# A fused attention and expert layer: few-row products padded to full height, and another stage order

## What is computed

```python
h = _L0_tok_ref(x, L0_tok_W, L0_tok_b, L0_tok_pos_emb)          # patches @ W.T + b + pos_emb
h = jnp.concatenate([h, txt], axis=1)                            # 249 tokens of 192
h = h + _L0_attn_ref(_layernorm(h, axis=-1), ...)                # 12 heads of 16, fq_act, log_int_softmax
h = h + _L0_ffn_ref(_layernorm(h, axis=-1), ...)                 # 16 experts of 128, 4 chosen, 1 shared
```

## Time and profile before

| | us |
|---|---|
| median of 3 runs | 3751.35 (3750.78 to 3755.88) |
| profiled execution, its own time | 3755.2 |
| span of the profile in it | 3753.5 |
| TensorE / VectorE / ScalarE / GpSimd busy | 3512.5 / 3529.2 / 3169.6 / 1378.5 |

### The profile page before, as it was taken

One profiled execution on the slowest core, in us unless ns is written; L12 is line 12 of the kernel. 1 busy time (PEld: TensorE's weight loads), 2 busy tenths in 40 slices (PEclk: granted clock), 3 DMA queues, 4 the chain that ended last, 5 costly groups with the idle time before them and its releaser, 6 DMA issues. The chain is left out here.

```text
span 3753.5 us, 97358 instructions
## 1 busy us (share of the span) xinstructions
PE 3512.5 (94%) x30764; PEld 2912.8 (78%) x30764; DVE 3529.2 (94%) x10282; ACT 3169.6 (84%) x6224; POOL 1378.5 (37%) x2219
## 2 busy tenths in 40 slices
PE   0269999999999999999999999999999999999999
PEld 0137888888888888888888888888888888888878
DVE  0579999999999999999999999999999999999995
ACT  0189889998998899899889989988998999899882
POOL 2033333434333343333334333333443343434330
PEclk9859999999999999999999999999999999999999
DMA  4100000000000000000000000000000000000000
GB/s 99 25 15 18 12 21 21 16 16 21 21 11 21 21 17 15 21 21 14 18 21 17 15 21 21 14 18 21 19 14 21 21 14 18 21 20 13 21 7 8
DMA packets 121213, 73.43 MB, mean 20 GB/s; under 512 B 15547, under 2 KB 118466, under 8 KB 120706
## 3 DMA queue, kind: packets, MB, share of 16 engines
q1 hardware_dynamic: 120706, 67.21, 7.1%
HBM read 54.89 MB, written 12.24 MB: 18 GB/s over the span
## 5 line engine op out<-in xcount | busy, mean ns | idle before, releaser
L1130 PE MATMUL pU<-x2T,UG 128*128 128x250 f16 x8704 | 1230.3, 270 | 0.3 <-DVE work L974 0.2
L1130 PEld LDWEIGHTS pU<-x2T,UG 128*128 128x128 f16 x8704 | 817.4, 97 | 124.3 <-DVE work L974 10.7
L1154 PE MATMUL pY<-WD,work 128*128 128x192 f32 (+1 forms) x4352 | 815.9, 329 | 0.0
L500 POOL TENSOR_SCALAR qz<-qk,quad,cst 128x249 bf16<-128x249 int8 x768 | 580.7, 769 | 549.5 <-ACT qk L605 541.7
L1154 PEld LDWEIGHTS pY<-WD,work 128*128 128x128 f32 (+1 forms) x4352 | 695.5, 187 | 20.9 <-DVE work L970 0.3
L913 DVE SCALAR_TENSOR_TENSOR work<-work,cst 128x249 f32<-128x249 f32 (+1 forms) x1536 | 676.7, 493 | 8.5 <-ACT work L576 7.5
L585 ACT ACTIVATE work<-work,alpha 128x249 f32<-128x249 f32 (+1 forms) x1536 | 643.7, 495 | 10.5 <-DVE work L934 3.3
L569 ACT ACTIVATE work<-a,room 128x249 bf16<-128x249 int8 (+1 forms) x1536 | 645.6, 504 | 0.8 <-POOL room L512 0.7
L1130 PE MATMUL pU<-x2T,UGB 67*128 67x250 f16 x2176 | 592.3, 272 | 0.0
L594 ACT ACTIVATE passing<-pX,cst 128x512 int16<-128x512 int16 (+3 forms) x768 | 475.6, 675 | 6.4 <-PE pO L1091 2.0
L512 POOL TENSOR_SCALAR room<-rmax,cst 128x4 f32<-128x4 f32 (+1 forms) x384 | 204.0, 531 | 745.2 <-DVE rmax L893 719.7
(11 more groups left out here) (201 smaller groups left out, 5832.8 us busy)
## 6 DMA issues: line engine op xcount, KB each, us to landing
img<-in_x_dram SPq DMA_DIRECT2D x896, 23.5 KB
img<-in_x_dram SPq DMA_DIRECT2D x768, 21.4 KB
h<-in_txt_dram SPq DMA_DIRECT2D x64, 96.0 KB, 1.9
out_dram<-yout SPq DMA_DIRECT2D x64, 96.0 KB
out_dram<-yout SPq DMA_DIRECT2D x64, 90.8 KB
WD<-in_L_ffn_Wd_dram SPq DMA_DIRECT2D x1, 1536.0 KB
work<-in_L_ffn_Wu_dram SPq DMA_DIRECT2D x2, 512.0 KB
work<-in_L_ffn_Wg_dram SPq DMA_DIRECT2D x2, 512.0 KB
```

Of the source, the lines that this page charges most:

```text
L500: nc_.tensor_scalar(qz[:, k * PER + m, :], qk8[:, k, :], quad[:, m:m + 1], cc(C_B0), ALU.mult, ALU.add)
L1130: a = mm(pU[:, s, q * EVEN:(q + 1) * EVEN], weights, x2T[i % 2][0:w, m, 0:EVEN], start=m == 0, stop=m == BLOCKS - 1)
L1154: a = mm(pY[0:n, t * 256:t * 256 + D], (act_[k % 2] if k else up[0])[:, c:c + n], WD[:, e, :], start=k == 0 and t == 0, stop=e == E - 1, s ...
```

## The change

It has two parts. First, products over few partitions are made products over more: `v_add`, `p_add` and `ones` become 128 partitions high (the added rows of `v_add` and `p_add` hold zeros, those of `ones` ones), `GW` gets a fourth block that holds the 64 last rows and zeros, so that `route` sums over 128 each time, and the last product of `embed` takes 116 partitions like the six ahead of it. GpSimd sets three more tensors to zero in the setup, and VectorE copies one more small block. `UGB` with its 67 partitions stays. Second, `ORDER` is another list with the same 251 stages. It was made from a table in which more stages may not stand beside GpSimd's. The list starts at another place of the cycle, so the shifts are one lower (down to -5).

```diff
-        v_add = sb("v_add", [SPLIT, D], BF16)
-        p_add = sb("p_add", [SPLIT, D], BF16)
+        v_add = sb("v_add", [P, D], BF16)
+        p_add = sb("p_add", [P, D], BF16)
...
-        ones = sb("ones", [SPLIT, P], BF16)
+        ones = sb("ones", [P, P], BF16)
...
-        GW = sb("GW", [P, 3, E], F16)
+        GW = sb("GW", [P, 4, E], F16)
...
-                      identf, ident, ident16, pick, ob, x2s, tokW_cols, UGB):
+                      identf, ident, ident16, pick, ob, x2s, tokW_cols, UGB, v_add, p_add, GW):
                 nc_.memset(a[:], 0.0)
...
+            link(ve.tensor_copy(GW[0:REST, 3, :], GW[0:REST, 1, :]))
...
-                            n = CROW + CK if 2 * c + 1 < K else CK
+                            n = CROW + CK
...
-                                w = P if m < BLOCKS - 1 else REST
-                                a = mm(pX[:, t * E:(t + 1) * E], x2T[i % 2][0:w, m, t * P:(t + 1) * P],
-                                       GW[0:w, (0, 1, 2, 0, 1)[m], :], start=m == 0, stop=m == BLOCKS - 1)
+                                a = mm(pX[:, t * E:(t + 1) * E], x2T[i % 2][:, m, t * P:(t + 1) * P],
+                                       GW[:, (0, 1, 2, 0, 3)[m], :], start=m == 0, stop=m == BLOCKS - 1)
```

More of the change, by code:

```diff
@@ L260, in fused_layer @@
         LATE_LOADS = E1 * SPLIT
-        VSETUP = 105
+        VSETUP = 106
         RT = 22
@@ L303, in fused_layer @@
         ORDER = [
[L304 to L352, removed]
+            ("imgload", 0, -1), ("gates", -4, -1), ("act", -5, 2), ("grow", -3, 1), ("mmU", -5, 4),
+            ("expo", -3, 3), ("turn", -2, 0), ("mmG", -5, 3), ("gate", -5, 3), ("turn", -2, 1),
@@ new lines, in fused_layer @@
+            ("low", -3, 3), ("quant", -2, 0), ("mmU", -5, 6), ("value", -3, 0), ("expo", -3, 5), ("qk", -2, 5),
+            ("share", -3, 4), ("value", -3, 1), ("qkq", -2, 5), ("r_top_pairs", -4, -1), ("top", -2, 0),
+            ("score", -2, 1), ("down", -5, 4), ("gate", -5, 5), ("silu", -5, 6), ("r_take_pairs", -4, -1),
+            ("grow", -3, 3), ("low", -3, 4), ("turnp", -3, 2), ("mmU", -5, 7), ("weigh", -3, 3),
+            ("quant", -2, 1), ("sum", -3, 5), ("pick", -5, 5), ("copyp", -3, 2), ("mmG", -5, 6), ("act", -5, 5),
@@ new lines, in fused_layer @@
+            ("turnp", -3, 3), ("peak", -2, 0), ("pick", -5, 6), ("alpha", -3, 5), ("r_penalty", -4, -1),
+            ("outq", -3, 0), ("score", -2, 2), ("outcast", -3, 0), ("below", -2, 0), ("copyp", -3, 3),
+            ("conv", -2, 2), ("down", -5, 5), ("top", -2, 1), ("quant", -2, 2), ("gate", -5, 6),
+            ("grow", -3, 4), ("mmG", -5, 7), ("quot", -2, 0), ("value", -3, 2), ("act", -5, 6),
+            ("r_masked", -4, -1), ("v", -2, -1), ("silu", -5, 7), ("top", -2, 2), ("weigh", -3, 4),
@@ new lines, in fused_layer @@
+            ("value", -3, 3), ("pick", -5, 7), ("share", -3, 5), ("peak", -2, 1), ("below", -2, 1),
+            ("mmU", -5, 8), ("u", -2, 0), ("vq", -2, -1), ("gate", -5, 7), ("square", -2, 0), ("peak", -2, 2),
+            ("low", -3, 5), ("mmG", -5, 8), ("power", -2, 0), ("turnp", -3, 4), ("r_top", -4, -1),
+            ("quot", -2, 1), ("grow", -3, 5), ("outq", -3, 1), ("act", -5, 7), ("down", -5, 6), ("u", -2, 1),
+            ("silu", -5, 8), ("power", -2, 1), ("copyp", -3, 4), ("pick", -5, 8), ("value", -3, 4),
@@ new lines, in fused_layer @@
+            ("weigh", -3, 5), ("turnp", -3, 5), ("gate", -5, 8), ("below", -2, 2), ("square", -2, 1),
+            ("down", -5, 7), ("mmG", -4, 0), ("r_take", -4, -1), ("score", -2, 3), ("mmU", -4, 0),
+            ("copyp", -3, 5), ("value", -3, 5), ("quant", -2, 3), ("expo", -2, 0), ("act", -5, 8),
+            ("quot", -2, 2), ("outcast", -3, 1), ("expo", -2, 1), ("top", -2, 3), ("down", -5, 8),
+            ("power", -2, 2), ("score", -2, 4), ("outq", -3, 2), ("outcast", -3, 2), ("sum", -2, 0),
@@ new lines, in fused_layer @@
+            ("silu", -4, 0), ("gate", -4, 0), ("project", -3, -1), ("mmU", -4, 1), ("score", -2, 5),
+            ("quant", -2, 4), ("result", -5, -1), ("peak", -2, 3), ("sum", -2, 1), ("prq", -3, -1),
+            ("residual", -3, -1), ("store", -5, -1), ("alpha", -2, 0), ("r_weight", -4, -1), ("down", -4, 0),
+            ("stats2", -3, -1), ("r_part0", -4, -1), ("below", -2, 3), ("quant", -2, 5), ("quot", -2, 3),
+            ("embed", -1, -1), ("mean2", -3, -1), ("top", -2, 4), ("silu", -4, 1), ("share", -2, 0),
@@ new lines, in fused_layer @@
+            ("spread2", -3, -1), ("r_rest", -4, -1), ("alpha", -2, 1), ("power", -2, 3), ("norm2", -3, -1),
+            ("low", -2, 0), ("r_part1", -4, -1), ("u", -2, 2), ("share", -2, 1), ("square", -2, 2),
+            ("mmG", -4, 1), ("peak", -2, 4), ("embed_h", -1, -1), ("txtload", 0, -1), ("r_part2", -4, -1),
+            ("chosen", -4, -1), ("copyw", -4, -1), ("stats", -1, -1), ("split2", -3, -1), ("top", -2, 5),
+            ("mmU", -4, 2), ("peak", -2, 5), ("turn2", -3, 0), ("grow", -2, 0), ("u", -2, 3), ("pick", -4, 1),
@@ new lines, in fused_layer @@
+            ("expo", -2, 2), ("mean", -1, -1), ("turn2", -3, 1), ("gate", -4, 1), ("weigh", -2, 0),
+            ("below", -2, 4), ("copy2", -3, 0), ("silu", -4, 2), ("mmU", -4, 3), ("spread", -1, -1),
+            ("copy2", -3, 1), ("square", -2, 3), ("act", -4, 1), ("route", -3, -1), ("sum", -2, 2),
+            ("logit", -3, -1), ("norm", -1, -1), ("below", -2, 5), ("quot", -2, 4), ("mmG", -4, 2),
+            ("pick", -4, 2), ("silu", -4, 3), ("split", -1, -1), ("alpha", -2, 2), ("turnp", -2, 0),
@@ L353, in fused_layer @@
+            ("u", -2, 4), ("lmax", -3, -1), ("copyp", -2, 0), ("gate", -4, 2), ("low", -2, 1),
+            ("below_max", -3, -1),
         ]
```

14 lines of the change are left out of this document (12 added, 2 removed).

## The result

The kernel with the change takes 3740.1 us (median of 10 runs, 3737.4 to 3745.3) against 3751.3 for the kernel before in the same session (10 runs, 3749.4 to 3755.9): a ratio of 0.997, 95% interval 0.9961 to 0.998. It is 11 us faster where 77 were forecast, and 0.1 us outside the range. Its profiled execution took 3745.3 us, with a span of 3743.6.

A forecast was written before the change was run, and what follows sets the result against it. VectorE was taken as the bound: 52.05 us plain work plus 1.1 of collisions and 0.25 of waits gave a 53.4 us period. 75 us over 61 periods, plus 3 for filling and emptying, less 1 setup: 3674 us, range 3620 to 3740.

The forecast's parts named there:

- What bounds the kernel: VectorE sets the 54.63 us period with 52.05 us of plain work; TensorE's 52.4 us leaves it 2.2 us of gaps.
- What is removed: Delays beside GpSimd's work, 2.5 us per image: `quot` 0.82, `power` 0.73, `expo` 0.55, small ones some 0.4.
- What is added: VectorE's collisions with GpSimd in the new order: 1.1 us per image taken, ends 0.3 and 2.5.
- a draw: `low1` and the subtraction of `split` both come about 1.1 us after `norm`; `low1` pays 0 to 0.70, 0.35 taken.
- wait at `spread`: `norm` waits for a power that `weigh0` can hold up: 0 to 0.70 us, 0.15 taken.
- the rival in which the collisions only move: `low1`, router operations and `norm` pay instead; 2.2 us remain, period 54.4, about 3735 us; chance 0.14.
- The lock: VectorE and GpSimd's shared port pair, held by the first for a whole instruction: accepted for the subtractions, denied for `conv`.
- The rival that had `low3` and `quot0` pay beside `conv`: The lock holds for `conv` too: up to 1.1 us per image more, period 54.5, about 3742 us; chance 0.04.
- The padding: Taller products save TensorE 0.78 us in `v` and `project`, 0.1 in `route` and `embed`; worth little by itself.
- The rival in which the padding gives nothing: Height changes don't make TensorE's gaps; VectorE waits 0.2 us more, about 3689 us; inside the forecast, no separate chance.
- The waits: VectorE waits more as TensorE's slack shrinks to 1.65 us, tightest at `embed_h`: 0.25 us added per period.
- the slower rival: TensorE reaches `embed` late, so VectorE waits 2 to 2.5 us at `embed_h`; 3802 us at 2.3; chance 0.08.

The follow-up runs named there:

- thin `conv`: The changed kernel with each `conv` on GpSimd doing one of its four multiplications, other heads' queries zero: 3703.47 us, ratio 0.9877 to the kernel before.
- the run with reciprocals: The changed kernel with `r_score`, `r_biased` and `r_pairs` on VectorE replaced by reciprocals at the same place: 3728.74 us, ratio 0.9943 to the kernel before.

## Why the prediction was wrong

**What bounds the kernel: right.** VectorE sets the period. The padding alone gave 2 us, and each of the five kernels that only took collisions away from the changed or the old one (thin `conv`, nine, five and one stage moved, three moved in the old order) had a shorter period.

**What is removed: right for the long operations.** `quot` and `power` were forecast at 530 to 560 and 405 ns and came to 495 to 531 and 401 to 407; together they freed 1.73 us where 1.55 were counted. `r_exp` freed 0.38. `expo` is another matter. It was to keep 0.29 us above its plain 9.6 and kept 0.63, against 0.56 before: the 0.3 of `expo0` beside `conv2` went, but `expo4`, which no term names, now stands beside `conv0` and pays 0.2.

**What is added: this step failed.** The sum taken for the new order was 1.1 us, with 2.5 as its upper end. What was paid is that upper end: the period is 54.51, and 54.51 - 52.05 = 2.5. By its terms:
- `low1`: 0.35 taken as a draw, 0.60 paid: the subtraction starts first, by 0.1 us in the timeline shown.
- `r_score` and `r_biased`: 0.15 taken with 0.5 as the bound; they paid 0.68, and `r_pairs`, which was not in the list of collisions, 0.33. The bound was called twice what `r_exp` pays, but `r_exp` pays 0.38 from start to start. And each of three operations in a row is held anew, for 0.2 to 0.3 us, and starts only when the one before it is done.
- `below_max`: 0.30, not counted. It stood behind `low1`, beside `vconv`.
- `r_part1` and `r_part2`: 0.31. The prediction saw them fall beside `split2` and gave them nothing.
- `sum` and `prq`: 0.29, where `sum` was to keep 0.05. Half is `sum5` beside a cast (0.38 us long in place of 0.16), half is `prq` with its reader directly behind it.
- `expo`: 0.34 more than forecast, as said.
- On the other side, `norm` did not wait at `spread` (0.15 taken), and four operations whose reader no longer follows directly saved 0.43 that no term has.

The moves test this list: without those collisions 2.4 us vanish from VectorE's rows and the time falls by 80 us. The prediction priced what a collision adds to a long operation and passed over most of the short ones, where an operation of 0.17 us pays 0.3. The true case is the rival in which the collisions only move (54.4 us, 3735), which had 0.14. That its number is so near is partly luck: of its terms `low1` came to 0.60 for 0.70, the router to 1.01 for 0.4, and `norm` to nothing for 0.5.

**The lock: read wrongly beside `conv`.** For the subtractions the trace agrees with the Trainium skill ("SBUF — State Buffer", "SBUF: two separate sides"): `low1` waits for the rest of one, as `quot3` and `power4` did. The prediction denied it for `conv` because `quot1` ran inside one at its plain 0.53 us. But the earlier trace rows show four multiplications merged into one row of 3.24 us. Taken singly, the one beside `quot1`, which starts 0.03 us behind it, lasts 0.85 where an undisturbed one lasts 0.55:

```profile
1006.71 0.85 POOL L500 TENSOR_SCALAR qz<-qk,quad,cst 128x249 bf16<-128x249 int8 x1
```

So VectorE was first and GpSimd waited, and the trace agrees with the rule there too. The same holds for `low3` (0.69, and 1.04 for the multiplication). Where GpSimd is first by 0.07 us or more, VectorE waits: the router's operations, `low3` in the run with reciprocals (0.98), `grow` in the one with nine moves (1.38). `r_exp`, 0.03 us behind a multiplication, takes 0.15 and is not held, and the multiplication takes 0.62. Reciprocals are not held (0.35 against 0.34). The rival that had `low3` and `quot0` pay beside `conv` (3742) is out all the same, though its number is near: both take their plain time after the change, `low3` because it gets in first, `quot0` because it stands beside no multiplication.

**The padding: the mechanism right, the size and the worth wrong.** It was to save 0.9 us of TensorE and saved 1.4: `v` and `project` gave 0.71 (0.78 forecast), `route` 0.34 and `embed` 0.34 (0.1 forecast for the two, on the ground that weight loads pace them; no run shows that). "Worth little by itself" holds in the old order (2 us). The rival in which the padding gives nothing was put at 3689, 15 us above the forecast; in the new order its absence costs 50 us. In that order `logit` waits for TensorE in each image. Rule for rule, the Trainium skill's "TensorEngine Tiling (Array Packing)" ("Key Properties"), where a change of mode drains the engine, gives the direction of all four kinds; that these products change the mode is inferred. In the trace the loss is 0.1 us each way around a 3-row product.

**The waits.** 0.25 us of new ones were added to the sum. After shows none: VectorE's idle time fell from 0.27 to 0.17 us of 56. The waits come only once the collisions are gone (0.57 us in the kernel with nine moves). Nor did `embed_h` ever wait as the slower rival had it; at most it waited 0.3 us, without the padding and with all moves.

**What stays open.** Which operations are held, and by which of GpSimd's, is known only for the pairs seen here. Where the rest of the gain goes in the kernels with nine and with three moves is read from timelines; no run took those causes away.

## What to carry to other kernels

Count every operation beside the other engine's work, the short ones first: one of 0.17 us waited for the rest of the other's instruction like a long one, so a chain of five short ones can pay more than one of 1.2 us. Look at both engines, instruction by instruction: an operation at its plain time may be the one that makes the other wait, and a shift of 0.1 us turns it round. Keep an operation and its reader apart. Try the parts of a change one at a time and together: here the padding alone is worth 2 us at most, the order alone costs 39, and both gain 11. And a new order is only as good as the trace of its own collisions: moving the nine stages that this trace showed as held gave seven times the gain of the whole change.

## What the runs showed of the hardware

- An undisturbed multiplication of `conv` takes GpSimd 0.55 us. A VectorE operation on 4 to 32 float32 elements that starts 0.07 us or more behind such an instruction, or behind a cast, ends 0.02 to 0.04 us after it: `r_biased` 0.50 us with 0.47 left, `sum5` 0.38 with 0.35 left, plain 0.16 to 0.18, with one input or two.
- Long ones wait as well: `low` 0.98 in place of 0.68 with 0.44 left of a multiplication, `grow` 1.38 in place of 1.18 with 0.35 left. A reciprocal of 32 elements (0.35, 0.34 elsewhere, with 0.47 left) and the reduction `r_sum` (0.19 with 0.32 left) did not wait.
- The other way round, when the two start within 0.03 us of each other, GpSimd's multiplication takes 0.85 beside `quot1` and 1.04 beside `low3`.
- VectorE starts 0.03 us after the end of an operation that it reads from, and some 0.08 us ahead of the end of one that it does not.
- Ten products of 16 columns took 0.60 us when two of them summed over 64 partitions and 0.25 when all summed over 128. Fourteen float32 instructions took 3.71 us with the last two over 52 partitions and 3.37 with all over 116.
